# A routed mixture-of-experts kernel on one core: experts kept in registers over the loop's turns, and a reordered start

## What is computed

```python
def _L0_cond_ref(x, w, W_base, b_base, As, Bs):
    out = jnp.einsum('btc,oc->bto', x, W_base) + b_base
    h = jnp.einsum('btc,erc->bter', x, As)
    lora = jnp.einsum('bter,eor,be->bto', h, Bs, w)
    return out + lora * SCALING
...
scores = jax.nn.softmax(x.astype(jnp.float32) @ gate_w.astype(jnp.float32).T, axis=-1)
topk_w, topk_i = jax.lax.top_k(scores, K)
topk_w = topk_w / (topk_w.sum(-1, keepdims=True) + 1e-20) * SCALE
combine = jnp.zeros((T, E), jnp.float32).at[jnp.arange(T)[:, None], topk_i].set(topk_w)
g = jax.nn.silu(jnp.einsum('td,edf->etf', x, w_gate)) * jnp.einsum('td,edf->etf', x, w_up)
expert_out = jnp.einsum('etf,efd->etd', g, w_down)
y = jnp.einsum('te,etd->td', combine, expert_out) + _swiglu_mlp(x, sw_gate, sw_up, sw_down)
```

## Time and profile before

| What | us |
|---|---|
| Three runs: median (lowest to highest) | 500.7 (499.16 to 501.32) |
| The profiled execution, its own time | 496.86 |
| Its span in the profile | 494.7 |
| TensorE busy | 487.9 (99%) |
| VectorE busy | 349.6 (71%) |
| ScalarE busy | 262.2 (53%) |
| GpSimd busy | 220.3 (45%) |

### The profile page before, as it was taken

How to read it: one execution, slowest core, us unless ns; L and a number is a source line. 1 busy time by engine, 2 the same in 40 slices (tenths; PEclk the granted TensorE clock), 3 DMA queues, 4 the chain that set the end, 5 groups by cost and what they waited for, 6 DMA issues and landing times.

```text
span 494.7 us, 9766 instructions
## 1 busy us (share of the span) xinstructions
PE 487.9 (99%) x3071; PEld 449.3 (91%) x3072; DVE 349.6 (71%) x783; ACT 262.2 (53%) x525; POOL 220.3 (45%) x231
## 2 busy tenths in 40 slices
PE   8999999999999999999999999999999999999996
PEld 7999988888888899999999999999999999888886
DVE  3557866888887556766876776676676666379895
ACT  3577876666563445565555554555555543535322
POOL 2052238655541453565776556555555652211100
PEclk9999999999999999999999999999999999999999
DMA  8398569472222244543444444444444451699932
GB/s 230 112 294 243 172 185 316 150 219 85 44 85 44 86 98 126 121 127 107 127 119 116 116 127 117 108 127 118 111 121 123 117 112 56 176 383 302 384 139 85
DMA packets 104936, 74.53 MB, mean 151 GB/s; under 512 B 61946, under 2 KB 99844, under 8 KB 104900
## 3 DMA queue, kind: packets, MB, share of 16 engines
q1 hardware_dynamic: 95780, 55.21, 38.5%
q0 software_dynamic: 6816, 18.62, 12.8%
q10 hardware_dynamic: 2304, 0.26, 0.5%
HBM read 40.25 MB, written 20.32 MB: 122 GB/s over the span
## 4 chain that ended last, share of the span: by engine, by line
PE 94%; DVE 3%; issue 1%; DMA 1%; ACT 1%; DVEq 0%
PE bank L281 23%; PE bank L282 22%; PE bank L283 22%; PE bank L800 10%; PE bank L802 5%; PE bank L772 5%; PE bank L586 2%; DVE acc L1369 1%; DMA xin<-in_x_dram 1%; PE bank L598 1%; PE bank L594 1%; PE bank L595 1%; ACT gt_h L962 1%; PE bank L722 1%; DVE bank L1258 1%
## 5 line engine op out<-in xcount | busy, mean ns | idle before, releaser
L561 POOL DMA_INDIRECT y_rows<-y_sb,dst_i x71 | 69.9, 985 | 82.8 <-DVE y_sb L1344 82.8
L281 PE MATMUL bank<-w_all,rt_h 128*128 x284 | 97.5, 343 | 0.0
L283 PE MATMUL bank<-w_all,rt_l 128*128 x284 | 91.6, 323 | 0.0
L282 PE MATMUL bank<-w_all,rt_h 128*128 x284 | 91.5, 322 | 0.0
L555 POOL DMA_INDIRECT rows<-x_halves,tok_i x71 | 68.6, 967 | 25.3 <-issue 21.1
L800 PE MATMUL bank<-w_all,gt_h 128*128 (+1 forms) x213 | 78.1, 397 | 0.1
L962 ACT CAST gt_h<-bank 128x512 fp32r<-128x512 f32 (+1 forms) x48 | 28.1, 585 | 86.5 <-DVE bank L1258 77.1
L281 PE MATMUL bank<-xs_h,sg_h 128*128 128x512 f32 x176 | 70.4, 400 | 0.0
L282 PE MATMUL bank<-xs_l,sg_h 128*128 128x512 f32 x176 | 68.9, 391 | 0.0
L283 PE MATMUL bank<-xs_h,sg_l 128*128 128x512 f32 x176 | 68.7, 390 | 0.0
L1331 DVE TENSOR_TENSOR g<-bank,act 128x352 f32<-128x352 f32 x71 | 37.2, 524 | 40.2 <-ACT act L983 38.8
(11 more groups left out here) (183 smaller groups left out, 1114.4 us busy)
## 6 DMA issues: line engine op xcount, KB each, us to landing
pick<-y_rows SPq DMA_DIRECT2D x16, 512.0 KB, 7.8
xin<-in_x_dram SPq DMA_DIRECT2D x8, 512.0 KB, 4.9
x_halves<-x_half SPq DMA_DIRECT2D x8, 512.0 KB, 3.3
w_own<-in_L_ffn_w_gate_dram SPq DMA_DIRECT2D x8, 352.0 KB, 4.3
w_own<-in_L_ffn_w_up_dram SPq DMA_DIRECT2D x8, 352.0 KB, 4.7
y_sb<-in_x_dram SPq DMA_DIRECT2D x5, 512.0 KB, 3.5
base_rows<-y_sb SPq DMA_DIRECT2D x5, 512.0 KB, 2.8
acc<-base_rows SPq DMA_DIRECT2D x5, 512.0 KB, 7.3
```

The source lines that it names most:

```text
L281: pe.matmul(o, lh, rh, start=start, stop=False, skip_group_check=skip)
L282: pe.matmul(o, lh, rl, start=False, stop=False, skip_group_check=skip)
L283: return pe.matmul(o, ll, rh, start=False, stop=stop, skip_group_check=skip)
L561: pool.indirect_dma_start(y_dram, bass.IndirectOffsetOnAxis(ap=dst_i[:, i:i + 1], axis=0), y_sb[:, i % 4, :], None).then_inc(s_sc[i % 4], 16)
```

## The change

- The expert of the running block and that of the one before are kept in two registers of TensorE (`kept`). A turn of the loop moves its last two experts there at its end and begins with copies of them (`as_kept`), and so do the blocks behind the loop. The load of the next turn's first expert moves into the last block of the turn before, and that for block 2 into block 1, ahead of the loop.
- The first 512 rows of x come as two transfers of two tiles (256 rows) each, with a semaphore each. Their turns go tile by tile, both halves k of a tile next to each other; tiles 0 and 1 need the first transfer alone.
- SyncE's order becomes x in two halves, W_base, the next rows of x, B (from ScalarE's queue), the broadcast b_base. g_raw and b_row go to ScalarE's queue.
- WARM is 12 instead of 14.

```diff
--- before.py
+++ after.py
@@ -38,6 +38,7 @@
 
     GT = 512
     TG = GT // P
+    HT = TG // 2
     NG = T // GT
     GB = GT // SEQ
 
@@ -52,7 +53,7 @@
     UP = NPRE + NBLK
 
     TURN = 12
-    WARM = 14
+    WARM = 12
 
     RANK_AT, HOT_AT = 4, 9
 
@@ -212,6 +213,7 @@
         s_cond, s_gate, s_ath, s_atl, s_wer = (sem(f"s_{n}") for n in ("cond", "gate", "ath", "atl", "wer"))
         s_wah, s_wal, s_bh, s_bl, s_bg = (sem(f"s_{n}") for n in ("wah", "wal", "bh", "bl", "bg"))
         s_xin = [sem(f"s_xin{i}") for i in range(2)]
+        s_xfirst = sem("s_xfirst")
         s_tx, s_txh, s_txl = sem("s_tx"), sem("s_txh"), sem("s_txl")
         s_H, s_hw, s_hwh, s_hwl = sem("s_H"), sem("s_hw"), sem("s_hwh"), sem("s_hwl")
         s_p, s_x1, s_half = sem("s_p"), sem("s_x1"), sem("s_half")
@@ -349,12 +351,16 @@
                     sp.wait_ge(s_rhi, i - 1)
                 sp.dma_start_transpose(turned[i % 2][:], rows[i % 3][:]).then_inc(s_turn[i % 2], 16)
 
-            load_x(0)
+
+            for h, got in enumerate((s_xfirst, s_xin[0])):
+                sp.dma_start(xin[0][:, h * HT:(h + 1) * HT, :],
+                             x_rows[h * HT * P:(h + 1) * HT * P, :].rearrange("(t p) d -> p t d", p=P)).then_inc(got, 16)
             sp.dma_start(base_raw[:], w_base.rearrange("(k p) c -> p k c", p=P)).then_inc(s_dw, 16)
-            sp.dma_start(g_raw[:], gate_w).then_inc(s_dg, 16)
-            sp.dma_start(b_row[:], b_base.rearrange("(k p) -> k p", p=P)).then_inc(s_dc, 16)
+            load_x(1)
+            for k in range(K):
+                sp.dma_start(b_raw[:, k, :].rearrange("p (e r) -> p e r", e=E),
+                             lora_b[:, k * P:(k + 1) * P, :].rearrange("e o r -> o e r")).then_inc(s_db, 16)
             sp.dma_start(bias[:, 0:D], b_base.rearrange("(a o) -> a o", a=1).broadcast_to([P, D])).then_inc(s_dbias, 16)
-            load_x(1)
             load_shared_gu(0)
             load_x(2)
             for i in range(NG):
@@ -621,7 +627,15 @@
             for k in range(K):
                 mm = pe.transpose(bank[7][:, k * P:(k + 1) * P], a_raw[:, k * P:(k + 1) * P], ident[:])
             mm.then_inc(s_aT, 1)
-            turn_x(0)
+
+            pe.wait_ge(s_xfirst, 16)
+            for t in range(TG):
+                if t == HT:
+                    pe.wait_ge(s_xin[0], 16)
+                for k in range(K):
+                    mm = pe.transpose(TX[k][:, t * P:(t + 1) * P], xin[0][:, t, k * P:(k + 1) * P], ident[:])
+                    if t == TG - 1:
+                        mm.then_inc(s_tx, 1)
             pe.wait_ge(s_dg, 16)
             for k in range(K):
                 pe.transpose(bank[6][:, k * E:(k + 1) * E], g_raw[:, k * P:(k + 1) * P], ident[0:E, 0:E])
@@ -809,19 +823,28 @@
                 e_down(i - 1, 1 - par, e_prev)
                 return e_next
 
+
+            kept = [pe.alloc_register(f"expert{n}") for n in range(2)]
+
+            def keep(*es):
+                for r, e in zip(kept, es):
+                    pe.reg_mov(r, pe.to_reg(e))
+
+            def as_kept():
+                return [pe.snap(r, min_val=0, max_val=E - 1) for r in kept]
+
             before = expert_of(0)
             expert = e_gate_up(0, 0, before, 1)
             down(*order[NPRE - 1])
-            e_step(1, 1, before, expert, None)
+            keep(expert, e_step(1, 1, before, expert, 2))
             n_turns = (NBLK - 3) // TURN
             with pe.Fori(0, n_turns) as q:
-                before = expert_of(q * TURN + 1)
-                expert = expert_of(q * TURN + 2)
+                before, expert = as_kept()
                 for s in range(TURN):
-                    before, expert = expert, e_step(
-                        q * TURN + (2 + s), s % 2, before, expert, q * TURN + (3 + s) if s + 1 < TURN else None)
+                    before, expert = expert, e_step(q * TURN + (2 + s), s % 2, before, expert, q * TURN + (3 + s))
+                keep(before, expert)
             i = n_turns * TURN + 2
-            before, expert = expert_of(i - 1), expert_of(i)
+            before, expert = as_kept()
             for n in range(i, NBLK):
                 before, expert = expert, e_step(n, n % 2, before, expert, None if n + 1 == NBLK else n + 1)
 
@@ -841,9 +864,8 @@
         def _(sc):
             sc.dma_start(a_raw[:], lora_a.rearrange("e r c -> (e r) c")).then_inc(s_da, 16)
             sc.dma_start(cond_in[:], cond).then_inc(s_dcond, 16)
-            for k in range(K):
-                sc.dma_start(b_raw[:, k, :].rearrange("p (e r) -> p e r", e=E),
-                             lora_b[:, k * P:(k + 1) * P, :].rearrange("e o r -> o e r")).then_inc(s_db, 16)
+            sc.dma_start(g_raw[:], gate_w).then_inc(s_dg, 16)
+            sc.dma_start(b_row[:], b_base.rearrange("(k p) -> k p", p=P)).then_inc(s_dc, 16)
 
             sc.wait_ge(s_ident, 1)
             sc.activation(spare[0:1, 2:3], ident[0:1, 0:1], ACT.Exp)
```

## The result

| What | before | changed |
|---|---|---|
| Median of 22 runs each, us | 500.64 | 497.48 |
| Lowest to highest | 497.01 to 504.61 | 493.84 to 506.19 |
| The profiled execution, its own time | 496.86 | 498.57 |
| Its span | 494.7 | 496.5 |

What follows compares the result with a forecast made beforehand. TensorE was taken as the bound, busy 487.9 of 494.7 us. Loop 2.15 plus start 0.4, queues nothing, gave 2.55 us off the 500.7 median: 498.1 us, range 496.2 to 500.6.

Steps and rivals of the forecast that it cites:

- The loop: Routed blocks' loop: stalls at entry, four jumps back and slower first turns of g all vanish, 2.15 us; lower end 0.
- Jump and two loads use up the lead; jump and moves don't: Loop boundaries: sequencer runs about 1.2 us ahead; jump plus two loads consume that, jump plus two to four register moves don't.
- at nothing: Loads moved into each turn's twelfth block and the block ahead of the loop: no cost, turns without stall staying 39.77 us.
- The start: First rows of x: fewer identity turns and two half transfers gain 0.4 us, ends 0 and 0.86.
- a's turns start at 4.05 instead of 4.51 ... a itself lands at 4.0, just in time: Kernel's head: two fewer identity turns at 0.23 each bring a's turns 0.46 us earlier, with a's transfer already landed.
- The first half at 4.3: Kernel's head: x's first 256 KB transfer lands at 4.3 us, between 4.0 and 5.5.
- What gives it back: Kernel's head: small turns at half clock cost 0.3 us; back-to-back casts of x hold gate_t to 7.4 to 7.6.
- The queues: Transfers moved between SyncE's and ScalarE's queues: no gain or loss taken; b late would at worst cost 0.5 us.
- Rival 3: SyncE's queue: b's 64-byte pieces land late, at 16.8 us, giving 503.5 us; chance 0.05, other queue mishaps included.
- Rival 1: Loop boundaries: the stall belongs to the jump, so stalls stay and only 0.4 is gained, 500.3 us; chance 0.13.
- Rival 2: Kernel's head: earlier clock or early halves give 0.86, with 2.15 making 3.0 in all, 497.7 us; chance 0.10.

Runs made afterwards that it cites:

- e1: Kernel before with only the changed loop (experts kept in registers): 494.14 against 496.17 us, ratio 0.9961.
- e4: Changed kernel with turns of six blocks instead of twelve, so ten jumps back instead of four: 493.26 us, ratio 0.9935 to before.
- e11: Kernel before with three loads at each turn's head, the second block's expert loaded there too: 501.58 against 500.28 us, ratio 1.0025.
- e13: Changed kernel with one of the two experts loaded at each turn's head, the other kept: 497.15 us, ratio 0.9939 to before.
- e2: Changed kernel with the loop of before, so the changed start alone: 495.88 against 496.17 us, ratio 0.9978.
- e9: Changed kernel run again unaltered beside before on another chip: 494.11 against 496.29 us, ratio 0.9957.
- e8: Changed kernel with b's transfers back on ScalarE's queue, g_raw and b_row on SyncE's: 498.41 against 500.28 us, ratio 0.9992.
- e7: Changed kernel with 2 identity turns instead of 12: 496.34 us, ratio 1.0 to before.

## Why the forecast held

**The loop: right in place and size.** Forecast 2.15, measured 2.03 by e1 (1.9 by its ratio, between 0.7 and 3.1) and 2.2 by its trace, with the jumps cleared by e4 and the loads convicted by e11 and e13. One step in its working was too simple: the loads were taken at their own durations. What counts is the pitch of 0.6 to 0.8 from one load's start to the next, and at the jumps back about one load of the two was already covered; at the entry it was not (0.41 with one load, 0.12 with none). "Jump and two loads use up the lead; jump and moves don't" held to the letter, and so did "at nothing" for the loads moved into the blocks: their turns are 39.64.

**The start: a term that is not confirmed.** 0.4 was taken, of 0 to 0.86; e2's medians give 0.3 and its ratio 1.1, the first profile 0.14 and e9's, where x's next turns start at 12.58 against 12.87, 0.29. But 12.87 is the latest of five profiles with before's start; against their median of 12.51 neither shows a gain. The forecast took the late clock of one profile, 1.87 for x's eight turns, as the rule for before, and didn't ask how it moves: three of the other four have 1.10. The total doesn't show this, since the loop carries most of it; that the sum came out near is in this part luck. The step that was off in the profiles of the change is "a's turns start at 4.05 instead of 4.51 ... a itself lands at 4.0, just in time": in the first profile A landed at 4.38 and its turns began at 4.42, 0.09 earlier than before, not 0.46; in e9 they began at 4.31. In other profiles with 12 identity turns they began at 4.08 to 4.26, so A's landing is a matter of the execution. "The first half at 4.3" couldn't be seen, since nothing waited for it: both halves were there when their turns' time came. x's last turn ended at 6.8, the later of the two ends given. "What gives it back" was right: the casts, now back to back, hold gate_t to 7.47 and 7.61, at the late end of "7.4 to 7.6", and L654 waits for it in these two.

**The queues: right that nothing is lost, short of the point.** The move of b was held to be neutral with a risk of 0.5. e8's profile shows the risk on the other side: where b stood before, it came late by 0.2, and x's next turns 0.3 after e9's. Rival 3, b late on SyncE's queue, is the opposite of what was found: there it took 5.0 to 5.9 us in all eight profiles.

**Rivals.** Rival 1 (the jump) is refuted. Rival 2 (the head gives more) is neither shown nor excluded: the first median fell near its 497.7, no profile of the changed kernel itself has the earlier clock that it needs, and e2's ratio allows it. By the medians the parts are 2.03 + 0.3 = 2.3, near e9's 2.18; by the ratios they are 1.9 + 1.1 = 3.0, near the first measurement's 3.1, and e9's own ratio gives 2.1. All lie within the intervals.

**What the forecast had not.** One execution moves by 3 us with the clock's rise and by as much with the waits for g, more than the change is worth. Both stand in profiles that were taken for the comparison of the two kernels: read alone, the first pair of profiles would have said 1.7 us slower.

## What to carry to other kernels

A load into a sequencer's register at a loop's head is free as long as the sequencer's lead covers it, and costs its full pitch from there on (here 0.6 to 0.8 us, twice its own common duration): carry values over the back edge, or load them in the middle of the long block before. The lead differs from place to place (one load was free at the jumps back and cost 0.29 at the entry), so measure it where the load stands. When a head is pulled forward, look at what was hidden by its lateness (here b's rows and the order of two casts), and compare it with several profiles of before. And where single executions differ by more than the gain, compare stretches of the loop and medians, never two profiles' spans.

## What the runs showed of the hardware that was not expected

- The clock's rise moves between executions of like starts. By the durations it comes at 6.5 to 7.4 us in six of the 14 profiles, before or within x's eight turns (1.10 to 1.42 us for them, so by about 6) in six, and at about 14 in e2's and e7's. With before's start alone, unchanged in five profiles, both 1.10 and 1.87 occur. Until the rise a pass of a three-pass product takes 0.22 us, from then on 0.12. The granted clock that the profiles give is 1.00 even where the durations are double (e2's, 7 to 12 us), so only the durations show it.
- With two turns of the identity instead of twelve the rise is at 13.8 us in the profile and the median 2.2 us higher.
- A register load from SBUF on TensorE's sequencer takes 0.30 us in the median of the 71 of the changed kernel, and up to 0.45 to 0.73 at the head of a turn or at the loop's entry in the others.
- b's two 64 KB transfers, in pieces of 64 bytes, take 5.0 to 5.9 us behind x and W_base on SyncE's queue (eight profiles), and 4.8 to 9.3 on ScalarE's, beside them (six profiles).
- VectorE and ScalarE at times start together 2 us late in the routed blocks (in 5 of the 14 profiles, before's not among them), at a cost of some 1.7 us each time. Cause open.
